# Local attention layers on one core: split norms, another order of the stages, and a narrower last MLP unit

## The chip, the cores and the metric

The kernel runs on one core of one Trainium2 chip. Its time is the device time of one execution in microseconds (us). The core has five engines that run side by side and meet only at semaphores: TensorE (PE, matrix products, with its weight loads as PEld), VectorE (DVE), ScalarE (ACT), GpSimd (POOL) and SyncE (SP, which issues transfers). A change of a few microseconds is small here: the three timed runs lie between 1883.65 and 1890.15 us.

## The reference

Four blocks follow one another on x of shape 16x128x256, each a cross attention and a feed-forward part, added to x with a gate. The change is in the feed-forward part of the second block, which is a small transformer of its own: two layers of local attention. It sees x as 16 sequences of 128 rows, which are one window each, so a row attends to itself and the rows before it in its sequence.

```python
def _layer(x, wqkv, qs, ksc, wo, lg, lb, w1, b1, w2, b2):
    h = shift_token(x)                       # second half of the columns comes from the row before
    q, k, v = jnp.split(h @ wqkv, 3, axis=-1)            # 8 heads of 64
    q = l2norm(q) * qs
    k = l2norm(k) * ksc
    q, k = rotary_xpos(q, k)
    o = local_attention(q, k, v)             # scores, masked softmax, values
    x = x + o @ wo
    h = shift_token(x)
    h = (h - mu) / jnp.sqrt(var + 1e-05) * lg + lb
    a, g = jnp.split(h @ w1 + b1, 2, axis=-1)            # 682 columns each
    x = x + (a * jax.nn.gelu(g, approximate=False)) @ w2 + b2
    return x
```

w1's gate and up columns are cut in units of 128, of which there are six; the last holds the 42 columns that are left (682 = 5 x 128 + 42).

## The kernel before

The whole network is one launch; x stays on the chip as `X`, 128 partitions x 16 blocks x 256 columns, in float32. The local layers are one phase, `local_layers` (line 1203 on), with tiles that carry the prefix L1f. A step is one block of 128 rows in one layer: 16 blocks times two layers are N = 32 steps.

The phase is a software pipeline written by hand. Each engine has a list of pieces with offsets, and `rounds` walks over t and calls each piece for step t + offset, in the order of the list; that order is what the engine executes, and semaphores hold it back where data or buffers are missing. Nothing else decides the order. In round t TensorE runs `queries_keys` of step t (two products of 128x512 into the two banks of psQ), `scores` of t-1 (into psS, a mask product and 8 heads), `turn_weights` of t-2 (transposes the softmax weights pr into psP), `values_in` of t, `values` of t-2 (weights times v, into psS bank 0), `turn_hidden` of t-3, `turn_in` of t+1, `output` of t-2 (into psB), `hidden` of t-3 in three groups j of two units (into psQ again, group j in bank j % 2), `down` of t-3 (psB), `shift`, and `turn` of t (transposes the rotated queries and keys, qr, into psP).

Between these, for step t: ScalarE squares the projections (`squares`, line 1472), VectorE sums the squares by head and clamps them (1580), GpSimd takes the power -0.5 (`roots`, 1287), VectorE multiplies (`norms`, 1597), GpSimd multiplies with the sines (`rotate`), VectorE with the cosines, and adds (`rotated`). ScalarE copies the turned queries and keys (`turned`, to qT and kT), and one step later takes the exponentials (`exps`, two groups of four heads, from maxima that VectorE takes in `tops`); VectorE sums them, GpSimd scales them, TensorE turns them, and ScalarE and VectorE copy one half each (`turned_weights`, pT). ScalarE copies the values' result (`outputs`, oT). For the MLP, ScalarE computes the gelu of a unit's gate (`gates`) and VectorE multiplies with the up part (`products`, into hid).

psQ serves the projections and the hidden units in turn, so the norms of step t must have read it before `hidden` of t-3 writes it:

```python
if j < 2:
    pe.wait_ge(s_qn, min(2 * t + 1 + j, 2 * N))
    after(pe, s_act, U * s.n)
else:
    pe.wait_ge(s_act, U * s.n + 2)
```

and `values` writes the psS bank that the exponentials of the next step read:

```python
pe.wait_ge(s_exp, min(2 * s.n + 3, 2 * N))
```

## Time and profile before

| | |
|---|---|
| Median of 3 runs | 1885.05 us (1883.65 to 1890.15) |
| Profiled execution | 1893.94 us, span 1892.1 us |
| Busy | PE 1654.8 (87%), PEld 1321.2 (70%), DVE 1128.7 (60%), ACT 955.8 (51%), POOL 908.8 (48%) |
| Hidden units' matmuls, L1419 | 1536 instructions, 182.0 us, 275 ns each |
| Query, key products, L1349 | 256, 122.2 us, 622 ns |
| Down projection, L1429 | 384, 94.3 us, 380 ns |
| Roots on GpSimd, L1290 | 32, 93.1 us, 2910 ns |
| Products of the MLP, L1631 | 192, 58.6 us, 346 ns |
| Gelu on ScalarE, L1512 | 192, 60.0 us, 364 ns |

The duration of a matmul is longer than its distance to the next, since matmuls are pipelined: what a group costs TensorE is read from the starts of groups. A matmul instruction on float32 stands twice in the trace for each one in the program. The busy share of an engine is its average over phases of different kinds; the local layers are one of them, and the rows below look at this phase alone.

### The profile page before, as it was taken

The page shows a single profiled execution, that of the slowest core. Times are in us where ns is not written, and L with a number is a line of the kernel's source. Part 1 is how long each engine was busy: PE and PEld are TensorE (multiplying, and loading weights), DVE is VectorE, ACT ScalarE, POOL GpSimd, SP SyncE. Part 2 cuts the span into 40 slices and gives each one's busy share as a digit, 9 for nine tenths or more (in the row PEclk, how much of TensorE's full clock was granted, in tenths as well). Part 3 has the DMA queues.
Part 4 walks back from the last instruction along what each step waited for, and adds up shares of the span by engine and source line. Part 5 has one row for each costly group of instructions (what it writes and reads, how often), then busy time and mean ns, then how long its engine had stood idle before and what let it go on. Part 6 is the DMA issues. An engine that isn't in the chain of part 4 may idle for free. (4 is left out here: it accounts for less than half of the span.)

```text
span 1892.1 us, 37858 instructions
## 1 busy us (share of the span) xinstructions
PE 1654.8 (87%) x11810; PEld 1321.2 (70%) x11841; DVE 1128.7 (60%) x3308; ACT 955.8 (51%) x2743; POOL 908.8 (48%) x1064
## 2 busy tenths in 40 slices
PE   6999369959749999999999999879976999939997
PEld 4777258848626777777777777768855888827775
DVE  4787536628745665666666666458864353327775
ACT  3776235514414655555565555357751355517761
POOL 2366545535445554555455455134755244466620
PEclk9999679979979999999999999989997999969999
DMA  4232355545120000000000000022424244332101
GB/s 153 86 118 90 119 169 171 169 168 182 38 99 1 2 1 1 1 1 1 1 1 1 1 1 1 1 75 86 150 105 174 71 128 129 115 111 98 53 7 45
DMA packets 74546, 138.43 MB, mean 73 GB/s; under 512 B 11568, under 2 KB 56880, under 8 KB 71920
## 3 DMA queue, kind: packets, MB, share of 16 engines
q1 hardware_dynamic: 59472, 95.22, 15.8%
q0 software_dynamic: 13728, 39.60, 6.1%
q8 instruction: 102, 1.67, 0.4%
q10 hardware_dynamic: 1152, 1.18, 0.2%
q14 instruction: 92, 0.75, 0.1%
HBM read 85.14 MB, written 50.82 MB: 72 GB/s over the span
## 5 line engine op out<-in xcount | busy, mean ns | idle before, releaser
L1419 PE MATMUL L1f_psQ<-L1f_xT,arena 128*128 128x128 f32 x1536 | 182.0, 275 | 0.9 <-ACT L1f_xT L1495 0.9
L1419 PEld LDWEIGHTS L1f_psQ<-L1f_xT,arena 128*128 128x128 f32 x1536 | 179.1, 192 | 2.8 <-ACT L1f_xT L1495 1.1
L1290 POOL TENSOR_TENSOR L1f_rn<-L1f_ss,L1f_root_c 128x16 f32<-128x16 f32 x32 | 93.1, 2910 | 176.6 <-DVE L1f_ss L1585 176.6
L1886 POOL DMA_INDIRECT outs_L2f<-L2f_tiles_ys,L2f_tiles_spot x79 | 75.4, 955 | 130.3 <-ACT L2f_tiles_ys L2025 130.3
L1305 POOL TENSOR_TENSOR L1f_rot<-L1f_qn,L1f_sinT 128x512 f32<-128x512 f32 x64 | 111.3, 1760 | 44.9 <-DVE L1f_qn L1602 44.9
L1349 PE MATMUL L1f_psQ<-arena,L1f_hT 128*128 128x512 f32 x256 | 122.2, 622 | 0.6 <-ACT L1f_hT L1502 0.6
L1512 ACT ACTIVATE L1f_sg<-L1f_psQ,vec1f 128x128 f32<-128x128 f32 x192 | 60.0, 364 | 121.3 <-PE L1f_psQ L1419 121.1
L1631 DVE SCALAR_TENSOR_TENSOR L1f_hid<-L1f_psQ,vec1f,L1f_sg 128x128 f32<-128x128 f32 x192 | 58.6, 346 | 84.3 <-ACT L1f_sg L1512 83.0
L1295 POOL TENSOR_TENSOR L1f_pr<-L1f_pr,L1f_rs 128x512 f32<-128x512 f32 x64 | 97.4, 1542 | 22.4 <-DVE L1f_rs L1595 22.4
L1583 DVE TENSOR_REDUCE L1f_ss<-L1f_sq 128x16 f32<-128x1024 f32 x32 | 39.0, 1220 | 114.3 <-ACT L1f_sq L1476 114.3
L1886 POOL DMA_INDIRECT outs_L0f<-L0f_tiles_ys,L0f_tiles_spot x79 | 75.8, 959 | 64.8 <-ACT L0f_tiles_ys L2025 64.3
L1476 ACT ACTIVATE L1f_sq<-L1f_psQ 128x512 f32<-128x512 f32 x64 | 38.2, 597 | 122.4 <-PE L1f_psQ L1349 122.4
L1429 PE MATMUL L1f_psB<-arena,L1f_hid 128*128 128x256 f32 x384 | 94.3, 380 | 1.1 <-DVE L1f_hid L1631 1.1
L714 ACT ACTIVATE L3x_pr<-L3x_psS,L3x_nmx 128x128 f32<-128x128 f32 x256 | 73.6, 432 | 32.8 <-DVE L3x_nmx L838 32.8
L1463 ACT ACTIVATE L1f_pr<-L1f_psS,L1f_mx 128x128 f32<-128x128 f32 x256 | 73.5, 382 | 30.4 <-DVE L1f_mx L1559 30.4
L2095 DVE COPY L2f_tiles_xT<-L2f_tiles_psT 128x256 f32<-128x256 f32 x79 | 33.5, 424 | 92.4 <-PE L2f_tiles_psT L1935 92.4
L1349 PEld LDWEIGHTS L1f_psQ<-arena,L1f_hT 128*128 128x128 f32 x256 | 51.3, 202 | 52.7 <-issue 50.2
L1946 PE MATMUL L0f_tiles_psH<-arena,L0f_tiles_xT 128*128 x316 | 83.8, 388 | 0.2 <-issue 0.2
L1965 PE MATMUL L2f_tiles_psY<-arena,L2f_tiles_aT 128*128 x316 | 81.4, 380 | 1.4 <-ACT L2f_tiles_aT L2019 1.4
L714 ACT ACTIVATE L0x_pr<-L0x_psS,L0x_nmx 128x128 f32<-128x128 f32 x256 | 74.8, 414 | 14.2 <-DVE L0x_nmx L838 14.1
L1946 PE MATMUL L2f_tiles_psH<-arena,L2f_tiles_xT 128*128 x316 | 81.4, 380 | 0.2 <-issue 0.2
L714 ACT ACTIVATE L2x_pr<-L2x_psS,L2x_nmx 128x128 f32<-128x128 f32 x256 | 75.4, 424 | 8.2 <-DVE L2x_nmx L838 8.2
(487 smaller groups left out, 4625.1 us busy)
## 6 DMA issues: line engine op xcount, KB each, us to landing
L0f_tiles_xs<-rows_L0f SPq DMA_DIRECT2D x79, 144.0 KB
L2f_tiles_xs<-rows_L2f SPq DMA_DIRECT2D x79, 144.0 KB
arena<-in_w_L2f SPq DMA_DIRECT2D x8, 1120.0 KB
arena<-in_w_L1f SPq DMA_DIRECT2D x8, 1088.0 KB, 7.4
L1x_got<-outs_L0f SPq DMA_DIRECT2D x16, 512.0 KB, 3.8
L3x_got<-outs_L2f SPq DMA_DIRECT2D x16, 512.0 KB, 3.6
arena<-in_w_L0f SPq DMA_DIRECT2D x8, 768.0 KB, 4.8
rows_L2f<-zero SPq DMA_DIRECT2D x31, 144.0 KB
```

The costliest lines, as they stand in the source:

```text
L714: ins = nc.scalar.activation(pr[:, s.p, g, j * P:(j + 1) * P], psS[:, g, j * P:(j + 1) * P], ACT.Exp, bias=nmx[:, s.p, 4 * g + j:4 * g + j ...
L1290: nc.gpsimd.tensor_tensor(rn[:, s.p], ss[:, s.p], root_c[:, :], ALU.pow).then_inc(s_rn, 1)
L1295: nc.gpsimd.tensor_tensor(a, a, rs[:, s.p, 4 * r:4 * r + 4].unsqueeze(2).broadcast_to([P, 4, P]), ALU.mult).then_inc(s_scaled, 1)
L1305: nc.gpsimd.tensor_tensor(to[:, :, i], of[:, :, o], sin, ALU.mult).then_inc(s_rot, 1)
L1349: mm = nc.tensor.matmul(out, hT[:, s.p, k], part(s, k * 3 * INNER + j * INNER, INNER), start=(k == 0), stop=(k == KC - 1))
L1419: mm = nc.tensor.matmul(out, w, xT[:, k], start=(k == 0), stop=(k == KC - 1), skip_group_check=True)
L1429: mm = nc.tensor.matmul(psB[:, 0:D], hid[:, u], part(s, UNITS_AT + u * UNIT_GLU + 2 * D, D), start=(u == 0), stop=(u == U - 1), skip_group ...
L1463: ins = nc.scalar.activation(pr[:, s.p, r, k * P:(k + 1) * P], psS[:, r, k * P:(k + 1) * P], ACT.Exp, bias=mx[:, s.p, h:h + 1])
L1512: nc.scalar.activation(sg[:, u], psQ[:, j % 2, 2 * i * P:(2 * i + 1) * P], ACT.Gelu, bias=column(s, 2 * KC + u)).then_inc(s_sg, 1)
L1886: nc.gpsimd.indirect_dma_start(r.outs, bass.IndirectOffsetOnAxis(spot[:, t % YR:t % YR + 1], 0), ys[:, t % YR], None).then_inc(r.s_out[t % ...
L1946: mm = nc.tensor.matmul(psH[:, t % 2, 0:W], xT[:, t % 2, k * P:(k + 1) * P], c.arena[:, bass.ds(cols[t] + (first + k * W), W)], start=(k = ...
L1965: mm = nc.tensor.matmul(psY[:, t % 2, 0:D], aT[:, t % 2, i * P:(i + 1) * P], c.arena[:, bass.ds(cols[t] + (first + 2 * W + i * D), D)], st ...
```

## The change

Four things change in the phase, and nothing outside it but the layout of the weights of the last unit.

The norms are taken in two halves: squares, their sums, the clamp, the roots and the multiplication run for the queries (w = 0) and the keys (w = 1) by themselves, with two semaphore counts a step where there was one.

The lists are reordered. TensorE starts a round with turning the weights and the scores, and the query and key projections come third. The lists of ScalarE and VectorE follow.

The result of the values is split: heads 0 to 3 go to psS, heads 4 to 7 to the first 256 columns of psB, and ScalarE copies each as it comes. `values` therefore also waits until VectorE has read the down projection's sum in psB.

The last unit's 42 gate and 42 up columns are packed in one block of 128 columns, gate from column 0 and up from column 64, so one product gives the gate in the partitions 0 to 63 and up in 64 to 127. ScalarE writes the gelu to the upper partitions, VectorE multiplies there, and the down projection reads 64 partitions. That product goes to psQ's bank 1, the other bank than that of unit 4, and has a semaphore count of its own.

```diff
+    LOWER, UPPER = slice(0, P // 2), slice(P // 2, P)
...
+    def unit_bank(u):
+        return 1 if u == U - 1 else u // 2 % 2
+
+    def unit_out(u, m, of=slice(0, P)):
+        at = 2 * (u % 2) * (u < U - 1) + m
+        return psQ[of, unit_bank(u), at * P:(at + 1) * P]
...
-            def roots(s):
-                pool.wait_ge(s_ss, 2 * s.n + 2)
+            def roots(s, w):
+                h = slice(w * LH, (w + 1) * LH)
+                pool.wait_ge(s_ss, 4 * s.n + 2 * w + 2)
                 after(pool, s_qn, 2 * s.n - 2)
-                nc.gpsimd.tensor_tensor(rn[:, s.p], ss[:, s.p], root_c[:, :], ALU.pow).then_inc(s_rn, 1)
+                nc.gpsimd.tensor_tensor(rn[:, s.p, h], ss[:, s.p, h], root_c[:, 0:LH], ALU.pow).then_inc(s_rn, 1)
...
-                after(pe, s_oT, s.n - 1)
+                after(pe, s_oT, 2 * s.n - 2)
...
             def values(s):
                 pe.wait_ge(s_exp, min(2 * s.n + 3, 2 * N))
                 pe.wait_ge(s_vx, s.n + 1)
+                after(pe, s_done, s.n - 1)
                 for k in range(4):
+                    to = psS[:, 0] if k < 2 else psB[:, :]
                     for r in range(2):
                         if k == 0:
                             pe.wait_ge(s_pT1 if r else s_pT0, s.n + 1)
                         h = 2 * k + r
-                        mm = nc.tensor.matmul(psS[64 * r:64 * r + 64, 0, k * P:(k + 1) * P], v[:, s.n % 3, h * LD:(h + 1) * LD],
+                        mm = nc.tensor.matmul(to[64 * r:64 * r + 64, (k % 2) * P:(k % 2 + 1) * P], v[:, s.n % 3, h * LD:(h + 1) * LD],
                                               pT[:, r, k * P:(k + 1) * P], start=True, stop=True, skip_group_check=True)
-                mm.then_inc(s_pv, 1)
+                    if k % 2:
+                        mm.then_inc(s_pv, 1)
...
-                pe.wait_ge(s_oT, s.n + 1)
+                pe.wait_ge(s_oT, 2 * s.n + 2)
...
                 if j < 2:
                     pe.wait_ge(s_qn, min(2 * t + 1 + j, 2 * N))
                     after(pe, s_act, U * s.n)
-                else:
-                    pe.wait_ge(s_act, U * s.n + 2)
                 for i in range(2):
-                    for m in range(2):
-                        out = psQ[:, j % 2, (2 * i + m) * P:(2 * i + m + 1) * P]
+                    if j == 2:
+                        pe.wait_ge(s_act, U * s.n + 2 + 2 * i)
+                    for m in range(1 if 2 * j + i == U - 1 else 2):
+                        out = unit_out(2 * j + i, m)
                         for k in range(KC):
                             w = part(s, UNITS_AT + (2 * j + i) * UNIT_GLU + (m * KC + k) * P, P)
                             mm = nc.tensor.matmul(out, w, xT[:, k], start=(k == 0), stop=(k == KC - 1), skip_group_check=True)
-                mm.then_inc(s_h, 1)
+                    if i == 1 or j == 2:
+                        mm.then_inc(s_h, 1)
...
-                    mm = nc.tensor.matmul(psB[:, 0:D], hid[:, u], part(s, UNITS_AT + u * UNIT_GLU + 2 * D, D),
+                    of = UPPER if u == U - 1 else slice(0, P)
+                    mm = nc.tensor.matmul(psB[:, 0:D], hid[of, u], part(s, UNITS_AT + u * UNIT_GLU + 2 * D, D)[of],
                                           start=(u == 0), stop=(u == U - 1), skip_group_check=True)
...
-            rounds([(queries_keys, 0), (scores, -1), (turn_weights, -2), (values_in, 0), (values, -2), (turn_hidden, -3),
+            rounds([(turn_weights, -2), (scores, -1), (queries_keys, 0), (values_in, 0), (values, -2), (turn_hidden, -3),
...
-            def squares(s):
-                after(act, s_ss, 2 * s.n)
-                for w in range(2):
-                    act.wait_ge(s_qk, 2 * s.n + w + 1)
-                    nc.scalar.activation(sq[:, w], psQ[:, w], ACT.Square).then_inc(s_sq, 1)
+            def squares(s, w):
+                after(act, s_ss, 4 * (s.n - 1) + 2 * w + 2 if s.n else 0)
+                act.wait_ge(s_qk, 2 * s.n + w + 1)
+                nc.scalar.activation(sq[:, w], psQ[:, w], ACT.Square).then_inc(s_sq, 1)
...
             def outputs(s):
-                act.wait_ge(s_pv, s.n + 1)
                 after(act, s_out, s.n)
-                nc.scalar.activation(oT[:, :].rearrange("p k t -> p (k t)"), psS[:, 0], ACT.Copy).then_inc(s_oT, 1)
+                for i, of in enumerate((psS[:, 0], psB[:, :])):
+                    act.wait_ge(s_pv, 2 * s.n + i + 1)
+                    nc.scalar.activation(oT[:, 2 * i:2 * i + 2].rearrange("p k t -> p (k t)"), of[:, 0:2 * P], ACT.Copy).then_inc(s_oT, 1)
...
-                act.wait_ge(s_h, 3 * s.n + j + 1)
                 for i in range(2):
                     u = 2 * j + i
-                    nc.scalar.activation(sg[:, u], psQ[:, j % 2, 2 * i * P:(2 * i + 1) * P], ACT.Gelu,
-                                         bias=column(s, 2 * KC + u)).then_inc(s_sg, 1)
+                    act.wait_ge(s_h, 4 * s.n + j + 1 + i * (j == 2))
+                    to, of = (UPPER, LOWER) if u == U - 1 else (slice(0, P), slice(0, P))
+                    nc.scalar.activation(sg[to, u], unit_out(u, 0, of), ACT.Gelu,
+                                         bias=column(s, 2 * KC + u)[of]).then_inc(s_sg, 1)
...
-            def squares(s):
-                dve.wait_ge(s_sq, 2 * s.n + 2)
-                after(dve, s_rn, s.n - 1)
-                nc.vector.tensor_reduce(ss[:, s.p], sq[:, :].rearrange("p w (h d) -> p (w h) d", d=LD), AXX, ALU.add).then_inc(s_ss, 1)
-                dve.wait_ge(s_ss, 2 * s.n + 1)
-                nc.vector.tensor_scalar(ss[:, s.p], ss[:, s.p], 1e-24, None, ALU.max).then_inc(s_ss, 1)
+            def squares(s, w):
+                h = slice(w * LH, (w + 1) * LH)
+                dve.wait_ge(s_sq, 2 * s.n + w + 1)
+                after(dve, s_rn, 2 * s.n - 2)
+                nc.vector.tensor_reduce(ss[:, s.p, h], sq[:, w].rearrange("p (h d) -> p h d", d=LD), AXX, ALU.add).then_inc(s_ss, 1)
+                dve.wait_ge(s_ss, 4 * s.n + 2 * w + 1)
+                nc.vector.tensor_scalar(ss[:, s.p, h], ss[:, s.p, h], 1e-24, None, ALU.max).then_inc(s_ss, 1)
...
-                dve.wait_ge(s_sg, U * s.n + 2 * j + 2)
                 for i in range(2):
                     u = 2 * j + i
-                    nc.vector.scalar_tensor_tensor(hid[:, u], psQ[:, j % 2, (2 * i + 1) * P:(2 * i + 2) * P], column(s, 2 * KC + U + u),
-                                                   sg[:, u], ALU.add, ALU.mult).then_inc(s_act, 1)
+                    dve.wait_ge(s_sg, U * s.n + (u + 1 if j == 2 else 2 * j + 2))
+                    of, m = (UPPER, 0) if u == U - 1 else (slice(0, P), 1)
+                    nc.vector.scalar_tensor_tensor(hid[of, u], unit_out(u, m, of),
+                                                   column(s, 2 * KC + U + u)[of], sg[of, u], ALU.add, ALU.mult).then_inc(s_act, 1)
...
+def glu_half_unit(gate, up, down):
+
+    n, h = gate.shape[1], P // 2
+    assert n <= h
+    gap = ((0, 0), (0, h - n))
+    both = np.concatenate([np.pad(gate, gap), np.pad(up, gap)], axis=1)
+    return np.concatenate([chunks(both), chunks(np.zeros_like(both)), np.pad(down, ((h, h - n), (0, 0)))], axis=1)
```

The first place is the order on TensorE from one round's projections to its output. Before, the names being psP for turned tiles, psS for scores and values, psA for the value projection, psQ for queries and keys:

```order
L1349 MATMUL L1f_psQ<-arena,L1f_hT 128x512 x4
L1328 MATMUL L1f_psS<-causal,ident 128x512 x2
L1333 MATMUL L1f_psS<-L1f_kT,L1f_qT 128x128 x8
L1344 MATMUL L1f_psP<-consts,L1f_pr 128x128 x8
L1349 MATMUL L1f_psA<-arena,L1f_hT 128x512 x2
L1370 MATMUL L1f_psS<-L1f_pT,L1f_v 64x128 x8
L1391 MATMUL L1f_psA<-consts,L1f_hn 128x128 x2
L1402 MATMUL L1f_psA<-consts,L1f_Y 128x128 x2
L1383 MATMUL L1f_psB<-arena,L1f_oT 128x256 x4
L1419 MATMUL L1f_psQ<-L1f_xT,arena 128x128 x16
```

Now, down to the same hidden groups:

```order
L1353 MATMUL L1f_psP<-consts,L1f_pr 128x128 x8
L1337 MATMUL L1f_psS<-causal,ident 128x512 x2
L1342 MATMUL L1f_psS<-L1f_kT,L1f_qT 128x128 x8
L1358 MATMUL L1f_psQ<-arena,L1f_hT 128x512 x4
L1358 MATMUL L1f_psA<-arena,L1f_hT 128x512 x2
L1381 MATMUL L1f_psS<-L1f_pT,L1f_v 64x128 x4
L1381 MATMUL L1f_psB<-L1f_pT,L1f_v 64x128 x4
L1403 MATMUL L1f_psA<-consts,L1f_hn 128x128 x2
L1414 MATMUL L1f_psA<-consts,L1f_Y 128x128 x2
L1395 MATMUL L1f_psB<-arena,L1f_oT 128x256 x4
L1431 MATMUL L1f_psQ<-L1f_xT,arena 128x128 x16
```

The turned weights and the scores have moved ahead of the four projection matmuls, and the eight products of the values are four into psS and four into psB.

The second place is the end of a round on TensorE: first down products, the shift, the third hidden group, the turn, the rest of down. Before:

```order
L1429 MATMUL L1f_psB<-arena,L1f_hid 128x256 x2
L1438 MATMUL L1f_psA<-L1f_Y,consts 128x128
L1419 MATMUL L1f_psQ<-L1f_xT,arena 128x128 x8
L1447 MATMUL L1f_psP<-consts,L1f_qr 128x128 x8
L1429 MATMUL L1f_psB<-arena,L1f_hid 128x256 x4
L1349 MATMUL L1f_psQ<-arena,L1f_hT 128x512 x4
```

Now:

```order
L1443 MATMUL L1f_psB<-arena,L1f_hid 128x256 x2
L1452 MATMUL L1f_psA<-L1f_Y,consts 128x128
L1431 MATMUL L1f_psQ<-L1f_xT,arena 128x128 x6
L1461 MATMUL L1f_psP<-consts,L1f_qr 128x128 x8
L1443 MATMUL L1f_psB<-arena,L1f_hid 128x256 x4
L1353 MATMUL L1f_psP<-consts,L1f_pr 128x128 x8
```

The third hidden group has six products where it had eight; the rest is as it was.

The third place is ScalarE's start of a round. Before (sq are the squares, pr the exponentials, pT the turned weights, v the values, oT their result):

```order
L1519 ACTIVATE L1f_kT<-L1f_psP 128x512
L1476 ACTIVATE L1f_sq<-L1f_psQ 128x512 x2
L1463 ACT_TABLE_LOAD
L1463 ACTIVATE L1f_pr<-L1f_psS,L1f_mx 128x128 x4
L1470 ACTIVATE L1f_pT<-L1f_psP 128x512
L1486 ACTIVATE L1f_v<-L1f_psA 128x512
L1481 ACTIVATE L1f_oT<-L1f_psS 128x512
L1495 ACTIVATE L1f_xT<-L1f_psA,vec1f 128x128 x2
```

Now:

```order
L1534 ACTIVATE L1f_kT<-L1f_psP 128x512
L1484 ACTIVATE L1f_pT<-L1f_psP 128x512
L1477 ACT_TABLE_LOAD
L1477 ACTIVATE L1f_pr<-L1f_psS,L1f_mx 128x128 x4
L1489 ACTIVATE L1f_sq<-L1f_psQ 128x512
L1477 ACTIVATE L1f_pr<-L1f_psS,L1f_mx 128x128 x4
L1489 ACTIVATE L1f_sq<-L1f_psQ 128x512
L1500 ACTIVATE L1f_v<-L1f_psA 128x512
L1495 ACTIVATE L1f_oT<-L1f_psS 128x256
L1495 ACTIVATE L1f_oT<-L1f_psB 128x256
```

The copy of the turned weights has moved from behind the exponentials to the head of the round, the squares stand one by one around the second group of exponentials, and that group has moved ahead of the values. The table loads are as many as before.

`norms` is split as `squares` is. VectorE's list follows in the same way: both maxima come first, and the sums, the clamp and the norms stand twice, in halves, with the weights' sums between them.

## Rows read from the trace of the kernel before

**Rows 1.** Busy time by stretch, two rounds: stretch, length, engines, clock, DMA.

```profile
607.55:628.30 20.75, 20.37 (x136) 15.67 (x136) 13.07 (x27) 11.75 (x28) 12.63 (x11) 1.00 0.00 1
...
1167.99:1188.54 20.55, 19.95 (x134) 15.27 (x134) 13.62 (x27) 11.82 (x27) 10.83 (x9) 1.00 0.00 1
```

**Rows 2.** Order of time, TensorE, one round: start, length, engine, line, operation.

```profile
898.17 3.60 PE L1349 MATMUL L1f_psQ<-arena,L1f_hT 128*128 128x512 f32 x8
901.82 0.38 PE L1328 MATMUL L1f_psS<-causal,ident 128*128 128x512 bf16 x1
902.13 1.16 PE L1333 MATMUL L1f_psS<-L1f_kT,L1f_qT 64*128 64x128 f32 x16
903.22 1.09 PE L1344 MATMUL L1f_psP<-consts,L1f_pr 128*128 128x128 f32 x8
904.15 1.88 PE L1349 MATMUL L1f_psA<-arena,L1f_hT 128*128 128x512 f32 x4
906.26 1.09 PE L1370 MATMUL L1f_psS<-L1f_pT,L1f_v 128*64 128x128 f32 x16 [0.23 <-ACT L1f_pT L1470]
...
907.57 0.38 PE L1402 MATMUL L1f_psA<-consts,L1f_Y 128*128 128x128 f32 x2
908.05 1.99 PE L1383 MATMUL L1f_psB<-arena,L1f_oT 128*128 128x256 f32 x8
909.88 3.73 PE L1419 MATMUL L1f_psQ<-L1f_xT,arena 128*128 128x128 f32 x32
...
914.53 1.95 PE L1419 MATMUL L1f_psQ<-L1f_xT,arena 128*128 128x128 f32 x16
916.32 1.04 PE L1447 MATMUL L1f_psP<-consts,L1f_qr 128*128 128x128 f32 x8
917.19 1.89 PE L1429 MATMUL L1f_psB<-arena,L1f_hid 128*128 128x256 f32 x8
```

**Rows 3.** Waits from 600 to 1180: total, times, longest.

```profile
PE L1f_psS L1370 <- ACT L1f_pT L1470: 6.6, 28, 0.2
```

**Rows 4.** Order of time, ScalarE and VectorE, the same round.

```profile
900.15 0.60 ACT L1476 ACTIVATE L1f_sq<-L1f_psQ 128x512 f32<-128x512 f32 x1 [2.48 <-PE L1f_psQ L1349]
...
903.77 0.69 DVE L1559 TENSOR_REDUCE L1f_mx<-L1f_psS 128x4 f32<-128x512 f32 x1
...
904.49 1.14 ACT L1463 ACTIVATE L1f_pr<-L1f_psS,L1f_mx 128x128 f32<-128x128 f32 x4 [0.79 <-DVE L1f_mx L1559]
...
905.51 0.61 ACT L1470 ACTIVATE L1f_pT<-L1f_psP 128x512 f32<-128x512 f32 x1
...
907.40 0.60 ACT L1481 ACTIVATE L1f_oT<-L1f_psS 128x512 f32<-128x512 f32 x1 [0.73 <-PE L1f_psS L1370]
...
908.73 0.28 ACT L1501 ACTIVATE L1f_hT<-L1f_psA 128x128 f32<-128x128 f32 x1
```

**Rows 5.** Groups by line and form, GpSimd: count, busy, mean ns, idle before.

```profile
L1290 POOL TENSOR_TENSOR L1f_rn<-L1f_ss,L1f_root_c 128x16 f32<-128x16 f32 x32 | 93.1, 2910 | 176.6 <-DVE L1f_ss L1585 176.6
...
L1313 POOL TENSOR_TENSOR L1f_rf<-L1f_vf,half 128x1 f32<-128x1 f32 x32 | 18.5, 577 | 2.7
...
L1281 POOL TENSOR_TENSOR rstd<-var,half 128x4 f32<-128x4 f32 x4 | 4.1, 1037 | 0.3
```

**Rows 6.** Groups by line and form, VectorE, 600 to 1180.

```profile
L1583 DVE TENSOR_REDUCE L1f_ss<-L1f_sq 128x16 f32<-128x1024 f32 x28 | 34.2, 1220 | 89.1 <-ACT L1f_sq L1476 89.1
```

**Rows 7.** Order of time, GpSimd and VectorE, the same round.

```profile
908.25 3.48 POOL L1305 TENSOR_TENSOR L1f_rot<-L1f_qn,L1f_sinT 128x512 f32<-128x512 f32 x2 [1.40 <-DVE L1f_qn L1602]
...
912.17 3.11 POOL L1295 TENSOR_TENSOR L1f_pr<-L1f_pr,L1f_rs 128x512 f32<-128x512 f32 x2 [0.44 <-DVE L1f_rs L1595]
...
913.17 1.22 DVE L1624 TENSOR_TENSOR L1f_qr<-L1f_cosd,L1f_rot 128x1024 f32<-128x1024 f32 x1
```

**Rows 8.** Order of time, start of the phase.

```profile
548.27 5.14 PE L1349 MATMUL L1f_psQ<-arena,L1f_hT 128*128 128x512 f32 x8
548.51 0.60 ACT L1519 ACTIVATE L1f_kT<-L1f_psP 128x512 f32<-128x512 f32 x1 [0.26 <-PE L1f_psP L1447]
```

More of the change, by code:

```diff
@@ L1313, in hidden_root @@
                 nc.gpsimd.tensor_tensor(rf[:, one], vf[:, one], c.half[:, :], ALU.pow).then_inc(s_rf, 1)
-            rounds([(row_roots, 4), (output_bias, -3), (roots, 0), (rotate, 0), (at(scaled, 0), -1), (at(scaled, 1), -1),
+            rounds([(row_roots, 4), (output_bias, -3), (at(roots, 0), 0), (at(roots, 1), 0), (rotate, 0), (at(scaled, 0), -1), (at(scaled, 1), -1),
                     (hidden_root, -2)])
@@ L1492, in affine @@
                 act.wait_ge(s_T, min(s.n + 5, N))
-                after(act, s_h, 3 * s.n)
+                after(act, s_h, 4 * s.n)
                 for k in range(KC):
@@ L1519, in turned @@
                     nc.scalar.activation(to[:, :].rearrange("p k t -> p (k t)"), psP[:, w], ACT.Copy).then_inc(done, 1)
-            rounds([(squares, 0), (at(exps, 0), -1), (turned_weights, -2), (values_in, 0), (outputs, -2), (affine, -3),
-                    (rows, 1), (at(exps, 1), -1), (gelu_table, -3), (at(gates, 0), -3), (at(gates, 1), -3), (at(gates, 2), -3), (turned, 0)])
+            rounds([(turned_weights, -2), (at(exps, 0), -1), (at(squares, 0), 0), (at(exps, 1), -1), (at(squares, 1), 0), (values_in, 0), (outputs, -2), (affine, -3),
+                    (rows, 1), (gelu_table, -3), (at(gates, 0), -3), (at(gates, 1), -3), (at(gates, 2), -3), (turned, 0)])
         @block.vector
@@ L1563, in turned_weights @@
                 dve.wait_ge(s_pt, 2 * s.n + 2)
-                after(dve, s_pv, s.n)
+                after(dve, s_pv, 2 * s.n)
                 nc.vector.tensor_copy(pT[:, 1], psP[:, 1]).then_inc(s_pT1, 1)
@@ L1595, in sums, with norms @@
                 nc.vector.reciprocal(rs[:, s.p], sm[:, s.p]).then_inc(s_rs, 1)
[L1597 to L1598 removed]
+            def norms(s, w):
                 after(dve, s_rot, 2 * s.n)
                 after(dve, s_cos, s.n)
[L1601 to L1604 removed]
+                dve.wait_ge(s_rn, 2 * s.n + w + 1)
+                nc.vector.tensor_tensor(qn[:, w], psQ[:, w].rearrange("p (h d) -> p h d", h=LH),
+                                        rn[:, s.p, w * LH:(w + 1) * LH].unsqueeze(2).broadcast_to([P, LH, LD]),
+                                        ALU.mult).then_inc(s_qn, 1)
             def output(s):
@@ L1646, in normed @@
                                             ALU.subtract, ALU.mult).then_inc(s_ln, 1)
-            rounds([(row_stats, 4), (results, -4), (squares, 0), (at(tops, 0), -1), (turned_weights, -2), (at(tops, 1), -1),
-                    (norms, 0), (at(weight_sums, 0), -1), (cosines, 0), (output, -2), (at(weight_sums, 1), -1),
-                    (sums, -1), (at(products, 0), -3), (rotated, 0),
+            rounds([(row_stats, 4), (results, -4), (turned_weights, -2), (at(tops, 0), -1), (at(tops, 1), -1), (at(squares, 0), 0),
+                    (at(weight_sums, 0), -1), (at(squares, 1), 0), (at(norms, 0), 0), (at(weight_sums, 1), -1), (sums, -1),
+                    (at(norms, 1), 0), (cosines, 0), (output, -2), (at(products, 0), -3), (rotated, 0),
                     (at(products, 1), -3), (shifted, -2), (at(products, 2), -3), (normed, -2), (rows, 2)])
@@ L2259, in layout @@
             [chunks(f["L1_ffn_wqkv"][n]), chunks(f["L1_ffn_wo"][n])]
-            + [glu_unit(w1[:, HID + a:HID + b], w1[:, a:b], w2[a:b]) for a, b in cuts], axis=1)
+            + [(glu_half_unit if b - a <= P // 2 else glu_unit)(w1[:, HID + a:HID + b], w1[:, a:b], w2[a:b]) for a, b in cuts],
+            axis=1)
+        half = np.zeros(P // 2, np.float32)
+        b_up = np.concatenate([b1[:cuts[-1][0]], half, b1[cuts[-1][0]:HID]])
+        b_up = np.pad(b_up, (0, UNITS1 * P - len(b_up)))
         d[f"col_L1f{n}"] = np.concatenate([columns(f["L1_ffn_ln_g"][n]), columns(f["L1_ffn_ln_b"][n]),
-                                           columns(np.pad(b1[HID:], (0, pad))), columns(np.pad(b1[:HID], (0, pad)))], axis=1)
+                                           columns(np.pad(b1[HID:], (0, pad))), columns(b_up)], axis=1)
         d[f"row_L1f{n}"] = np.concatenate([f["L1_ffn_b2"][n], f["L1_ffn_q_scale"][n], f["L1_ffn_k_scale"][n]])
```

10 lines of the change are left out of this document (2 added, 8 removed).

## The prediction

> **What bounds the kernel now.** The change touches one phase only, the local layers, which fill the span from about 529 to 1230 us. I read it from the outside in. First the busy time by stretch: a round of this phase, one step of each stage on different row blocks, takes 20.75 us, and TensorE is busy in 20.37 us of it at full clock (1.00), while VectorE is busy 13.07, ScalarE 11.75 and GpSimd 12.63 us [rows 1]. Then the order of time on TensorE alone [rows 2]: the starts of its groups add up to the round with hardly a gap, so every matmul taken away shortens the round, and a change on the other engines counts only where TensorE stands before it. Then the waits: the view names one that TensorE still has in every round, 0.23 us before the values' matmuls [rows 3]; a second shows in the starts of rows 2, before the output projection. Last, what the other engines do around these two [rows 4], and how long the operations take that the change splits [rows 5, 6]. Round 4 starts at 607.55 and the last full round ends at 1188.54 [rows 1]: 28 rounds in this steady state.
>
> **The change on TensorE, part by part.**
> (1) The last unit of the MLP has 42 of 128 columns in use. Its gate and up columns now share one block, so that unit needs one product where it had two. A float32 product over two chunks is 4 matmul instructions. The third hidden group has 16 of them, from 914.53 to 916.32, 0.112 us each [rows 2]; 12 remain: -0.45 us. The down projection of that unit reads 64 partitions in place of 128, but as many instructions of as many columns (8 in 1.73 us, 0.215 each), so I give it no gain.
> (2) The wait before the values. The four instructions of the value projection start at 904.15 and take 0.43 each (8 took 3.44, from 898.17 to 901.61), so TensorE could go on at 905.87; it goes on at 906.26 [rows 2], 0.39 later. What it waits for is pT, which ScalarE copies at 905.51, behind the four exponentials of 904.49 [rows 4]. In the new order TensorE turns the weights first, ScalarE copies them first, and scores and query/key products (1.61 + 3.44 us) lie between the turn and the values. That wait goes: -0.39 us.
> (3) The wait before the output projection. The turn of 907.57 has two instructions of 0.11, done at 907.79; the output starts at 908.05, when oT (907.40 to 908.00) is out [rows 2, 4]. With oT in halves, the first is copied while the second half of the products runs. Price of a half: 128x128 takes 0.28 and 128x512 takes 0.60 [rows 4], so some 0.39. The second half starts 1.14 us after the values' start as the whole does now and ends 0.39 later in place of 0.60: -0.2 us, and about 0.05 of the wait stays.
> (4) An added cost. The down projection's last product now has a 64-row form between 128-row ones. The trace has such a change already: the last mask product starts at 901.82 and is over after 0.215, at 902.03, but the 64-row scores start at 902.13, 0.10 later; the way back to 128 rows (903.22) shows no gap [rows 2]. I add 0.10; the ends are 0 and 0.33.
> The Trainium skill ("TensorEngine Tiling (Array Packing)", Key Properties) says that changing the tiling mode drains the engine. A full drain would be what a 256-column product lasts over its spacing, 0.379 less 0.215, so 0.165 us on the way in and as much on the way out. The trace shows 0.10 and nothing; by that rule the sum below would be 6 us smaller, and it is the second case.
> Sum of a round: -0.45 - 0.39 - 0.20 + 0.10 = -0.94 us, 19.81 in place of 20.75.
>
> **Do the other engines keep up with 19.8?** I set the new round at 0 where the weights are turned, with the spacings of rows 2: scores 0.93, queries and keys 2.54, values' projection 5.98, values 7.70, output 9.26, hidden one and two 11.09 (32 instructions of 0.112: 3.57), third hidden 15.74, turn 17.08, rest of down 17.95, end 19.8. Scores are done 1.68 after their start, 2.61. The two maxima take 0.69 each [rows 4], to 3.95. Exponentials one: 3.4 to 4.5. The first square can start 1.98 after its product starts (898.17 to 900.15), at 4.5, the second at 6.2; exponentials two lie between. The reductions of 512 columns take what a maximum takes, 0.69, or half of the 1.22 of now [rows 6], and the clamp is a small one: they land at about 6.1 and 7.65.
> The root of 8 columns is in no row. Roots of 1, 4 and 16 columns take 0.575, 1.04 and 2.91 us [rows 5], a straight line of about 0.42 + 0.155 a column, so 1.65 for 8; the ends are 1.04 and 2.91. With 1.65 the roots are out at 7.9 and 9.5, and the second norm at 10.3. Norms one and two are wanted by hidden one (11.09) and two (12.9): slack 2.5 us and more. Rotation (3.48) runs 10.4 to 13.9 [rows 7]. The sum of 1.22 stands behind the first products and starts now 3.29 after hidden one (913.17 against 909.88), so 14.4 to 15.6, and the turn wants it at 17.08: slack 1.4. The second products are over some 0.7 later, at 16.3; the last unit, alone in the other bank, wants them after its neighbour's 8 instructions, at 16.65: slack 0.35, the tightest place. The weights' scaling (3.11) ends at 17.0 for a turn at 19.8, and kT's copy at about 19.0. The values' first wait, the exponentials one, is over at 4.5 for 7.7. VectorE's busy time grows by two small instructions and stays near 13.5, ScalarE's and GpSimd's below 13: none of them can be the bound by its load, only by its order.
>
> **Start and end of the phase.** In rounds 0 to 3 the chain projection, squares, roots, norms, rotation, turn sets the time, with TensorE idle most of it. The split takes from this chain one half reduction (0.55), one root less a half (2.91 - 1.65 = 1.26) and one norm (0.6): 2.4 us a round. But scores now stand ahead of the projections, and they need kT, which is copied only at 548.51 to 549.11, where the next projection starts at 548.27 [rows 8]: about 0.9 for kT and 1.6 to 2.5 for the scores (the clock is half there) from round 1, and 1 to 2 more for the weights' turn from round 2. That is -2.4, about +0.5, +2 and +2: I count 0, with 3 us either way. In the three rounds after 1188.54 the 0.45 of part 1 comes three times, the wait does not (the exponentials are just as late): -1.3.
>
> **Sum.** 28 x 0.94 = 26.3, plus 1.3, is 27.6, so 28 us off. The profiled execution took 1893.94 us (span 1892.1), 8.9 above the median of 1885.05; the rest of the program is unchanged, and the same 28 us come off both: 1866 for a profile, 1857 for the median.
>
> **Rivals.**
> - Part of it is lost at the 64-row form: 0.33 in place of 0.10 a round, saving 0.71 x 28 + 1.3 = 21: 1864. For it: only one such change could be read, and the new one comes between long products. Against: the gap there is 0.10.
> - The change doesn't do what it says, since the wait moves on: xT is made behind two copies in place of one (slack 0.8 to hidden one), the last unit stands behind the second products (0.35), kT at the new head of the round (0.8). One of them late beyond its slack by half a microsecond or more leaves 0 to 0.45 a round: 1872 to 1885. For it: three slacks under 1 us, each at the end of several estimates. Against: the matmuls that go are gone in any case.
> - Slower: the roots. If 8 columns cost as much as 16 (2.91), both roots end at 12.0, the second norm at 12.7, rotation at 16.2, the sum at 17.5, the second products at 18.2, and the last unit's product waits from 16.65 until then: 1.55 us more than the 0.94 gained, so +0.6 x 28 = +17: 1902. It decides from 2.1 us a root (the slack of 0.35 and the 0.5 by which rotation ends before the sum starts, over two roots), and no gain is left from 2.55. For it: GpSimd's operations have a fixed part that the trace shows only through fits. Against: the 4-column root at 1.04.
> - More than I count: the ramp's chains gain (2.4 us x 4) and the 64-row weights load beside the running product: 1850.
>
> **How the numbers follow.** Forecast 0.68, its own range 1852 to 1863; 64-row form 0.10; moved wait 0.10; slower 0.07; more 0.05. A measurement here tells about 0.3% (5.7 us) from no change. Faster is the first two, the last and half of the moved wait: 0.88; the other half of it, 0.05, is no change; slower 0.07. The range 1849 to 1870 leaves out the slower case and most of the moved wait.
>
> **What would show it.** Right: rounds of about 19.8 us, TensorE busy over 98% of them; 12 instructions in the third hidden group; no idle time before the values; the output's start within 0.1 us of the turn's end; roots of 128x8 at 1.6 to 1.7 us; scores 0.93 us behind the turned weights. Wrong: a wait of TensorE for hid or kT, a root above 2.1 us, a gap over 0.2 us around the last down product, or rounds 1 to 3 longer by more than 2 us each.

## The result and the profile after

The changed kernel takes 1875.40 us (median of 5 runs, 1870.42 to 1876.58) against 1885.05 (5 runs by now, 1883.65 to 1890.15). The ratio of the two is 0.9925, with a 95% interval of 0.9906 to 0.9943: faster by 14 us (11 to 18). The two medians alone lie 9.7 us apart. By the one it is half of the 28 forecast, by the other a third, and both are outside the range of 1849 to 1870. The profiled executions differ by 17.3 us (span 1892.1 and 1874.8), of which 16.0 lie between the first projection of the local layers and the first matmul of the next phase (704.4 and 688.4 us). Outside the phase, where nothing was changed, the profile after is 3.3 us longer ahead of it and 4.6 us shorter behind it. So a difference of a few microseconds in the whole time says little, and the change is read from the phase.

Busy time in a round of the changed kernel, columns as in [rows 1]:

```profile
613.61:633.80 20.19, 20.19 (x134) 15.11 (x133) 13.50 (x28) 12.30 (x29) 13.10 (x11) 1.00 0.00 1
```

A round is 20.19 us in place of 20.75, and TensorE is busy throughout: 20.19 of 20.19. The view of waits names no wait of TensorE between 600 and 1160 us; the 0.23 before the values [rows 3] is gone. So by its records TensorE never stands idle now, and still the round is not the 19.81 of the forecast. The order of time on TensorE says where it is, against [rows 2]:

```profile
896.27 1.09 PE L1353 MATMUL L1f_psP<-consts,L1f_pr 128*128 128x128 f32 x8
897.20 0.59 PE L1337 MATMUL L1f_psS<-causal,ident 128*128 128x512 bf16 x2
897.72 1.16 PE L1342 MATMUL L1f_psS<-L1f_kT,L1f_qT 64*128 64x128 f32 x16
898.81 3.70 PE L1358 MATMUL L1f_psQ<-arena,L1f_hT 128*128 128x512 f32 x8
902.35 1.88 PE L1358 MATMUL L1f_psA<-arena,L1f_hT 128*128 128x512 f32 x4
904.16 0.66 PE L1381 MATMUL L1f_psS<-L1f_pT,L1f_v 128*64 128x128 f32 x8
...
905.19 0.44 PE L1403 MATMUL L1f_psA<-consts,L1f_hn 128*128 128x128 f32 x2
905.46 0.38 PE L1414 MATMUL L1f_psA<-consts,L1f_Y 128*128 128x128 f32 x2
905.74 1.99 PE L1395 MATMUL L1f_psB<-arena,L1f_oT 128*128 128x256 f32 x8
907.57 3.73 PE L1431 MATMUL L1f_psQ<-L1f_xT,arena 128*128 128x128 f32 x32
...
912.23 1.50 PE L1431 MATMUL L1f_psQ<-L1f_xT,arena 128*128 128x128 f32 x12
913.57 1.04 PE L1461 MATMUL L1f_psP<-consts,L1f_qr 128*128 128x128 f32 x8
914.44 2.09 PE L1443 MATMUL L1f_psB<-arena,L1f_hid 128*128 128x256 f32 x8
916.46 1.09 PE L1353 MATMUL L1f_psP<-consts,L1f_pr 128*128 128x128 f32 x8
```

What counts are the distances from one start to the next, in us:

| Stretch | Before | After | Difference |
|---|---|---|---|
| Turned weights | 0.93 | 0.93 | 0 |
| Mask and scores | 1.61 | 1.61 | 0 |
| Queries and keys | 3.44 | 3.54 | +0.10 |
| Values' projection, to the values' start | 2.11 | 1.81 | -0.30 |
| Values | 1.03 | 1.03 | 0 |
| The turns into psA, to the output's start | 0.76 | 0.55 | -0.21 |
| Output, hidden one and two, first down, shift | 6.48 | 6.49 | 0 |
| Third hidden group | 1.79 | 1.34 | -0.45 |
| Turn | 0.87 | 0.87 | 0 |
| Rest of down | 1.73 | 2.02 | +0.29 |
| Sum | 20.75 | 20.19 | -0.56 |

(The sums are of the starts; single entries are rounded.) The rest of down has as many matmuls as before, of as many columns, and takes 0.29 us more. What happens there shows on the weight loads of the same place:

```profile
895.64 0.29 PEld L1443 LDWEIGHTS L1f_psB<-arena,L1f_hid 64*128 64x128 f32 x2 [0.33 <-issue]
896.26 0.86 PEld L1353 LDWEIGHTS L1f_psP<-consts,L1f_pr 128*128 128x128 f32 x8 [0.33 <-issue]
```

The 64-row loads of the last unit come 0.33 us after the end of the load before them, and the next 128-row load comes 0.33 us after the end of those. The profile puts no engine to these gaps, and hid was long done: VectorE's last two products stand at 893.66 to 894.40. A gap alone proves little, since the loads of the 512-column products stand 0.24 apart too. What differs is that both loads here start with their own matmul (895.64 and 896.26, the matmuls at 895.64 and 896.27). In the dense stream elsewhere a load starts while the matmul before its own still runs.

The matmuls of that place one by one, each from a window that holds only it:

```profile
895.33 0.38 PE L1443 MATMUL L1f_psB<-arena,L1f_hid 128*128 128x256 f32 x1
895.64 0.48 PE L1443 MATMUL L1f_psB<-arena,L1f_hid 64*128 64x256 f32 x1
895.96 0.38 PE L1443 MATMUL L1f_psB<-arena,L1f_hid 64*128 64x256 f32 x1
896.27 0.33 PE L1353 MATMUL L1f_psP<-consts,L1f_pr 128*128 128x128 f32 x1
```

Instructions of 256 columns otherwise start 0.215 apart. Here the distances are 0.31, 0.32 and 0.31, and the second of the transposes starts 0.16 behind the first (at 896.43), where the others of its group are 0.11 apart. So each change of form delays two starts: the first instruction of the new form by 0.10, and the second by 0.10 as well, or 0.05 where it is a transpose of 128 columns. That makes 0.29 in the rest of down and 0.05 in the group behind it.

Roots of 8 columns on GpSimd:

```profile
L1299 POOL TENSOR_TENSOR L1f_rn<-L1f_ss,L1f_root_c 128x8 f32<-128x8 f32 x56 | 92.8, 1658 | 178.5 <-DVE L1f_ss L1601 177.4
```

1.66 us each, where 1.65 was read off the line through [rows 5].

The start of the phase went the other way: it became longer. From the first projection to the end of round 3 it takes 81.5 us (532.11 to 613.61) in place of 78.7 (528.81 to 607.55). The end, from the end of round 31 to the next phase, takes 41.6 us in place of 44.6. With 28 rounds of 0.56: +2.8 - 15.7 - 3.0 = -16.0, the whole of the phase's difference.

### The profile page after: what moved, and what is told of

It is laid out like the page before. It is cut to its first block and busy times, and to the rows that moved or that the text cites. A ratio compares the mean times of both kernels' runs of the same rounds, so it can differ in the third digit from the quotient of the medians.

```text
span 1874.8 us, 37913 instructions
## 1 busy us (share of the span) xinstructions
PE 1658.0 (88%) x11713; PEld 1311.1 (70%) x11713; DVE 1144.0 (61%) x3372; ACT 974.5 (52%) x2775; POOL 922.1 (49%) x1096
## 3 DMA queue, kind: packets, MB, share of 16 engines
q8 instruction: 101, 1.65, 0.4%
## 5 line engine op out<-in xcount | busy, mean ns | idle before, releaser
L1299 POOL TENSOR_TENSOR L1f_rn<-L1f_ss,L1f_root_c 128x8 f32<-128x8 f32 x64 | 105.9, 1656 | 213.0 <-DVE L1f_ss L1601 211.8
L1431 PE MATMUL L1f_psQ<-L1f_xT,arena 128*128 128x128 f32 x1408 | 167.7, 275 | 0.9 <-ACT L1f_xT L1509 0.9
L1431 PEld LDWEIGHTS L1f_psQ<-L1f_xT,arena 128*128 128x128 f32 x1408 | 164.8, 192 | 2.8 <-ACT L1f_xT L1509 1.1
L1443 PE MATMUL L1f_psB<-arena,L1f_hid 128*128 128x256 f32 (+1 forms) x384 | 99.7, 388 | 0.0
L1358 PEld LDWEIGHTS L1f_psQ<-arena,L1f_hT 128*128 128x128 f32 x256 | 47.4, 195 | 53.0 <-issue 48.5
L1599 DVE TENSOR_REDUCE L1f_ss<-L1f_sq 128x8 f32<-128x512 f32 x64 | 43.9, 686 | 56.2 <-ACT L1f_sq L1489 56.2
L1443 PEld LDWEIGHTS L1f_psB<-arena,L1f_hid 128*128 128x128 f32 (+1 forms) x384 | 65.2, 190 | 15.6 <-issue 9.6
```

The lines of the kernel that those rows point to most:

```text
L1299: nc.gpsimd.tensor_tensor(rn[:, s.p, h], ss[:, s.p, h], root_c[:, 0:LH], ALU.pow).then_inc(s_rn, 1)
L1358: mm = nc.tensor.matmul(out, hT[:, s.p, k], part(s, k * 3 * INNER + j * INNER, INNER), start=(k == 0), stop=(k == KC - 1))
L1431: mm = nc.tensor.matmul(out, w, xT[:, k], start=(k == 0), stop=(k == KC - 1), skip_group_check=True)
L1443: mm = nc.tensor.matmul(psB[:, 0:D], hid[of, u], part(s, UNITS_AT + u * UNIT_GLU + 2 * D, D)[of], start=(u == 0), stop=(u == U - 1), skip_ ...
```

## The experiments

Two theories stand for the missing 0.38 us a round. A: TensorE loses the early load of its weights each time that it changes between products with 64 and with 128 rows or columns of weights, and the narrow unit's 64-row product adds two such changes. B: that product waits for its own data, the last gelu and product, which cross from one half of the partitions to the other. Eight kernels were run in two groups, each beside the kernel before on its own chip. The kernel before has a median of 1870.78 us in the first group (full rows, the old order with 64 rows, the norms in one piece, the old start) and 1871.95 in the second (the other four). So ratios count and not times across chips, and an expected time that starts from 1875 is some 14 us too high for these chips.

**Full rows.** The last unit's down product reads all 128 partitions; the lower half is zero.

```diff
+            nc.gpsimd.memset(hid[LOWER, U - 1], 0.0).then_inc(s_one, 1)
-                    of = UPPER if u == U - 1 else slice(0, P)
-                    mm = nc.tensor.matmul(psB[:, 0:D], hid[of, u], part(...)[of],
+                    mm = nc.tensor.matmul(psB[:, 0:D], hid[:, u], part(...),
```

(Arguments of `part` left out; the memset has a semaphore count of its own, which the engines wait for at the start.)

> The changed kernel, with the last unit's down product over all 128 partitions (the lower half of hid for that unit is set to zero once), so TensorE never leaves the 128-row form there. Theory A (each change between the 64-row and the 128-row form keeps the next weight load from going ahead): the rest of down is back from 2.02 to 1.73 us and the turn of the weights behind it from 0.93 to 0.87; a round is 20.19 - 0.29 - 0.06 = 19.84 us, 28 rounds give 9.8 us, the time is some 10 to 11 us under the changed kernel's 1875, so 1865. Rival B (the product waits for the last unit's own gelu and product, which come late): the rows in use change nothing, a round stays 20.19 and the time 1875. Rival C (my forecast's price, 0.10 for the form): round 20.09, time 1872.

Measured: 1847.62 us, ratio 0.9875 (0.9860 to 0.9891). TensorE in order of time:

```profile
881.14 1.89 PE L1443 MATMUL L1f_psB<-arena,L1f_hid 128*128 128x256 f32 x8
882.87 1.04 PE L1354 MATMUL L1f_psP<-consts,L1f_pr 128*128 128x128 f32 x8
...
900.12 1.04 PE L1461 MATMUL L1f_psP<-consts,L1f_qr 128*128 128x128 f32 x8
900.99 1.89 PE L1443 MATMUL L1f_psB<-arena,L1f_hid 128*128 128x256 f32 x8
```

The rest of down is 1.73 again (881.14 to 882.87), a round 19.85 (881.14 to 900.99), as theory A said to 0.01. So the 64-row form costs 0.34 us a round in the changed kernel. The phase is 10.2 us shorter than there (678.2 and 688.4), and the two ratios, 0.9875 and 0.9925, lie some 9 us apart, where 10 to 11 were expected. The gelu and product of the last unit are unchanged and cross the partitions as before, so theory B falls.

**The narrow unit in the old order**, with 64 rows and with full rows: the kernel before with only the last unit changed.

> The kernel before with the narrow last unit alone (one product for gate and up, down over 64 rows), old order, norms whole. Theory A: a round is 20.75 - 0.45 + 0.29 = 20.59 us, so 4 to 6 us under the kernel before. Rival C (0.10 for the form): 20.40, 10 us under it. Rival B (a late last unit): near 20.6 too, but with a wait of TensorE on hid in the waits.

Measured, one run: 1869.72 us, where the runs of the kernel before lie between 1868.83 and 1873.14; the 4 to 6 us that were expected did not come. TensorE:

```profile
886.57 1.50 PE L1427 MATMUL L1f_psQ<-L1f_xT,arena 128*128 128x128 f32 x12
887.91 1.04 PE L1457 MATMUL L1f_psP<-consts,L1f_qr 128*128 128x128 f32 x8
888.78 2.09 PE L1439 MATMUL L1f_psB<-arena,L1f_hid 128*128 128x256 f32 x8
890.80 3.70 PE L1357 MATMUL L1f_psQ<-arena,L1f_hT 128*128 128x512 f32 x8
...
894.86 1.16 PE L1341 MATMUL L1f_psS<-L1f_kT,L1f_qT 64*128 64x128 f32 x16
```

Against [rows 2]: third hidden group 1.34 (-0.45), rest of down 2.02 (+0.29), projections with mask, to the scores, 4.06 in place of 3.96 (+0.10). A round is 20.70, so the narrow unit by itself gives 0.05 us of its 0.45 (3.4 us over the phase, 701.0 and 704.4). I had expected 20.59: that the projections behind the 64-row product lose another 0.10 was not in it. A wait of TensorE for hid, the sign of theory B, stands in 2 rounds only, 0.5 us in all.

> The kernel before with the narrow last unit alone, and its down product over all 128 partitions. Theory A (the change of form eats the narrow unit's gain): the 0.45 us come through, a round is 20.30 us where the same with 64 rows had 20.70, so some 13 us under the kernel before, 0.7%. If something else in the narrow unit costs (its gelu across partitions, its own waits), the round stays near 20.7.

Measured: 1857.64 us, ratio 0.9927 (0.9907 to 0.9947). The rounds:

```profile
881.38 1.89 PE L1439 MATMUL L1f_psB<-arena,L1f_hid 128*128 128x256 f32 x8
883.11 3.60 PE L1358 MATMUL L1f_psQ<-arena,L1f_hT 128*128 128x512 f32 x8
...
887.07 1.16 PE L1342 MATMUL L1f_psS<-L1f_kT,L1f_qT 64*128 64x128 f32 x16
```

The rest of down takes 1.73, the projections 3.44, to the scores 3.96; a round is 20.31 (20.33 in the mean of rounds 5 to 31), as expected. The same unit that was worth 0.05 us a round with 64 rows is worth 0.44 with 128, half of them zeros, and 0.7% of the time.

**Two units with 64 rows.** In the changed kernel, unit 2's down product too reads its upper half only. Unlike the last unit, unit 2 has values in its lower half, and this kernel leaves them out of the sum; it serves for the time alone.

```diff
-                    of = UPPER if u == U - 1 else slice(0, P)
+                    of = UPPER if u in (2, U - 1) else slice(0, P)
```

> The changed kernel with a second 64-row product in each down projection: unit 2's too reads only its upper 64 partitions (the lower half of that unit's sum is left out). As many matmuls of as many columns. Theory A: one more stretch in the 64-row form costs what the first does, 0.3 us before a 128-row weight load of a like group, so a round is 20.19 + 0.29 = 20.48 us, and the rest of down takes 2.31. Rival (the 0.29 belongs to the end of the round, or to the last unit's data): 20.19.

Measured: a round of 20.58, 0.39 more than the changed kernel, where 0.29 were expected; the one timed run took 1875.49 us, beside 1871.95 for the kernel before.

```profile
890.42 1.04 PE L1461 MATMUL L1f_psP<-consts,L1f_qr 128*128 128x128 f32 x8
891.39 2.38 PE L1443 MATMUL L1f_psB<-arena,L1f_hid 64*128 64x256 f32 x8
893.71 1.09 PE L1353 MATMUL L1f_psP<-consts,L1f_pr 128*128 128x128 f32 x8
```

The rest of down is 2.32, as expected, and the turn ahead of it 0.97 in place of 0.87. Read one by one, unit 2's product delays four starts by 0.10 each: its own two (891.39, which lengthens the turn, and 891.71) and the first two of the 128-row form behind it (892.02 and 892.34). I expected 0.29 since I had counted the rest of down alone; the fourth delay falls in the group behind, where it is 0.05 to 0.06 on the last unit's transposes and 0.10 on unit 3's products. So the cost comes again with a second product in another place, and the 0.29 belongs neither to the end of the round nor to the last unit's data. Two 64-row products side by side were not tried: no run separates the number of changes from the number of 64-row products. Both products also read the upper half, so nothing here tells whether a lower half would cost the same.

**Norms in one piece.** The changed kernel with sums, roots and norms whole, behind the second square.

```diff
-            rounds([..., (at(roots, 0), 0), (at(roots, 1), 0), (rotate, 0), ...
+            rounds([..., (roots, 0), (rotate, 0), ...
-  (at(weight_sums, 0), -1), (at(squares, 1), 0), (at(norms, 0), 0), (at(weight_sums, 1), -1), (sums, -1), (at(norms, 1), 0),
+  (at(weight_sums, 0), -1), (squares, 0), (at(weight_sums, 1), -1), (sums, -1), (norms, 0),
```

> The changed kernel with sums, roots and norms in one piece again, behind the second square. If the split is what keeps the norms off TensorE's path in the new order: the norms end 0.8 us after the first hidden group wants its bank, a round is 20.19 + 0.85 = 21.0 us and the time about 1895 to 1900, over the kernel before. Rival (there is slack enough, the split pays only at the start): round 20.19, 5 to 7 us more in rounds 0 to 3.

Measured, one run: 1931.06 us, 60 over the kernel before; a round is 22.42, where 21.0 was expected. VectorE, then TensorE:

```profile
895.30 1.29 DVE L1616 TENSOR_TENSOR L1f_qn<-L1f_psQ,L1f_rn 128x512 f32<-128x512 f32 x2 [2.20 <-POOL L1f_rn L1298]
...
900.24 2.05 DVE L1638 TENSOR_TENSOR L1f_qr<-L1f_cosd,L1f_rot 128x1024 f32<-128x1024 f32 x1 [0.69 <-POOL L1f_rot L1313]
```

```profile
893.35 1.99 PE L1394 MATMUL L1f_psB<-arena,L1f_oT 128*128 128x256 f32 x8
896.10 3.81 PE L1430 MATMUL L1f_psQ<-L1f_xT,arena 128*128 128x128 f32 x32 [0.75 <-issue]
...
900.83 1.06 PE L1430 MATMUL L1f_psQ<-L1f_xT,arena 128*128 128x128 f32 x8
902.86 0.71 PE L1430 MATMUL L1f_psQ<-L1f_xT,arena 128*128 128x128 f32 x4 [0.97 <-DVE L1f_hid L1646]
```

The norms end at 896.59, and the hidden groups start at 896.10, after the first of the two, in place of some 895.2: 0.9 lost. (The profile writes "issue" at this wait; that it is for the norms is read from the program and from the times.) The sum for the turned queries and keys then waits for rotation, the second products stand behind it on VectorE, and the last unit waits another 1.15 for them (901.71 to 902.86). I expected the first wait (0.85) and not the second. The split of the norms, which takes no work from TensorE, is what carries the new order: without it the rest of the change is 1.67 us a round slower than the kernel before.

**Values in one bank.** The kernel with full rows, with the values' result in one bank and its copy whole.

> The kernel with full rows, with the values' result in one bank and one copy again. If halving the copy is what took 0.20 us from the wait before the output projection: a round is 19.85 + 0.20 = 20.05 us, with the output's start 0.48 after the turn's in place of 0.28. Rival (the copy is early anyway, since ScalarE has less to do there in the new order): 19.85.

Measured, one run: 1851.13 us, a round of 20.06, 0.21 more than with full rows and as expected. TensorE and ScalarE:

```profile
891.24 0.38 PE L1412 MATMUL L1f_psA<-consts,L1f_Y 128*128 128x128 f32 x2
891.73 1.99 PE L1393 MATMUL L1f_psB<-arena,L1f_oT 128*128 128x256 f32 x8
```

```profile
890.04 0.60 ACT L1496 ACTIVATE L1f_v<-L1f_psA 128x512 f32<-128x512 f32 x1 [1.06 <-PE L1f_psA L1359]
891.08 0.60 ACT L1491 ACTIVATE L1f_oT<-L1f_psS 128x512 f32<-128x512 f32 x1 [0.44 <-PE L1f_psS L1380]
```

The output starts 0.49 after the turn again, at the end of one copy of 0.60. The halves are worth 0.21 us a round.

**The old order in rounds 0 to 3.** Full rows, and for t < 4 the lists of the kernel before on TensorE, ScalarE and VectorE, with the norms split.

```diff
-                for fn, off in pieces:
+                for fn, off in (first if first and t < 4 else pieces):
```

> As the kernel with full rows, and in rounds 0 to 3 the pieces of TensorE, ScalarE and VectorE stand in the order of the kernel before (the norms stay split). The changed kernel needs 81.5 us from the first projection to the end of round 3, the one before 78.7. Theory S (the scores and the turned weights ahead of the projections lengthen the start): 81.5 falls to 71 to 76, below the one before, since the split norms take 2.4 us out of each chain; the time is 5 to 9 us under the kernel with full rows. Rival T (the start is longer by chance of the clock, which is half there): no change beyond 1 us.

Measured: 1834.62 us, ratio 0.9816 (0.9802 to 0.9829). In the changed kernel the first rounds go like this on TensorE:

```profile
547.44 1.97 PE L1461 MATMUL L1f_psP<-consts,L1f_qr 128*128 128x128 f32 x8 [5.98 <-DVE L1f_qr L1639]
550.18 1.01 PE L1337 MATMUL L1f_psS<-causal,ident 128*128 128x512 bf16 x2 [0.78 <-ACT L1f_kT L1534]
551.12 2.08 PE L1342 MATMUL L1f_psS<-L1f_kT,L1f_qT 64*128 64x128 f32 x16
553.13 4.47 PE L1358 MATMUL L1f_psQ<-arena,L1f_hT 128*128 128x512 f32 x8
```

Between the turn and the projections stand a wait of 0.78 for kT and 2.95 us of mask and scores, which take 1.61 in the steady rounds. TensorE has been idle for 6 us before, and the granted clock of these 2.95 us is 0.50, the lower of its two levels of 1.2 and 2.4 GHz, where the steady rounds have 1.00:

```profile
550.18:553.13 2.95, 2.95 (x18) 1.90 (x18) 0.00 (x0) 0.00 (x0) 0.00 (x0) 0.50 0.00 0
```

With the old start, in order of time:

```profile
534.97 1.97 PE L1461 MATMUL L1f_psP<-consts,L1f_qr 128*128 128x128 f32 x8 [5.98 <-DVE L1f_qr L1644]
536.73 4.57 PE L1359 MATMUL L1f_psQ<-arena,L1f_hT 128*128 128x512 f32 x8
541.35 0.38 PE L1338 MATMUL L1f_psS<-causal,ident 128*128 128x512 bf16 x1
```

The projections follow the turn at once. It is they that now run in part at the lower clock (0.79 on average from 536.73 to 541.35), and the scores behind them have 1.00. To the end of round 3 it takes 71.2 us (519.79 to 591.02) in place of the changed kernel's 81.5, and 7.5 less than the kernel before: the split norms shorten the chain there, as forecast, and the new order had cost all of that and 2.8 more. Theory S holds, and rival T, which allowed no more than 1 us, falls.

The time fell by more than the start explains: 13.0 us by the medians of the two kernels with full rows, 11 by their ratios, where 5 to 9 were expected. The profiles show 8.5 us in the phase (678.2 and 669.7); the rest lies outside it, where the two kernels are the same, and is not explained.

**Scores ahead of the turned weights**, on top of that.

> The kernel with full rows and the old start, with the scores ahead of the turned weights, so that the group behind the 64-row scores is the transposes (which take 0.93 there and 0.87 elsewhere) and not the projections (3.54 there and 3.44 elsewhere). Theory A: 0.10 - 0.06 = 0.04 us a round, 19.81, 1 us in all, which the time can't tell but the rounds can. Rival (exponentials and squares come too late, since ScalarE's first copy now stands behind them): a round over 20 us with a wait for hid or pT.

Measured: 1835.19 us, ratio 0.9810 (0.9792 to 0.9828), so the same as the last; the round is 19.80 where it was 19.85, and 19.81 was expected. No wait of TensorE appears. TensorE:

```profile
889.37 1.09 PE L1354 MATMUL L1f_psP<-consts,L1f_pr 128*128 128x128 f32 x8
890.30 3.60 PE L1359 MATMUL L1f_psQ<-arena,L1f_hT 128*128 128x512 f32 x8
893.73 1.88 PE L1359 MATMUL L1f_psA<-arena,L1f_hT 128*128 128x512 f32 x4
```

The projections are back at 3.43, and the turned weights, now behind the scores, take 0.93 where they took 0.87. So a group of transposes behind the scores is 0.06 longer, and a group of 512-column products there 0.10.

The last two kernels take 1.8% to 1.9% off the kernel before, where the change took 0.75%; their phase is 34.7 and 38.0 us shorter than before, against 16.0.

## Why the prediction was wrong

**Step 4, the price of the 64-row form, failed.** The prediction put it at 0.10 us a round, and the runs show 0.34: with full rows the round falls from 20.19 to 19.85. It took the 0.10 from the one change of form that it read, into the scores [rows 2], where it saw only the first late start, and it read the way out as free. One by one, the second score also starts late there (902.34 behind 902.13, 0.21, where the later pairs are 0.11 apart). On the way out the first of the turned weights stands 0.21 behind the last pair of scores (903.01 and 903.22), and the second 0.17 behind the first. "The way back to 128 rows shows no gap" was the mistake: a late start does not show as idle time, since a matmul's record is longer than its distance to the next; it is the distance that grows, and the turned weights' 0.93 against the turn's 0.87 for the same number of transposes was there to be read.

The Trainium skill ("TensorEngine Tiling (Array Packing)", Key Properties) says that a change of mode drains the engine. The page gives no duration; the prediction's estimate of a drain in and out from its own rows was 0.33, and the trace agrees in sum, with 0.34, though not in the parts, 0.20 in and 0.15 out for 0.165 each. I had that case with a chance of 0.10, and it would have given 21 us, still more than was measured, so it was not the whole of the miss.

**Step 2 was half right.** The wait for pT went entirely, but the stretch fell by 0.30 and not by 0.39. The values start 0.52 behind the last instruction of their projection (903.64 to 904.16), where those are 0.43 apart, and their load starts with them (904.16). That looks like another such change, into 64 columns, which the wait had covered; no run takes it away, so this 0.09 is read by likeness and not shown by an experiment. The new order has a price that no step had: behind the scores the projections lose 0.10, where the turned weights lost 0.06 before, 0.04 net. The three make the missing 0.24 + 0.09 + 0.04, which is 0.38 but for rounding, 10.6 us in 28 rounds.

**Steps 1 and 3 held**: -0.45 and -0.21. So did the other engines: no wait of TensorE is left, the roots take 1.66, and the price of a 128x256 copy was 0.38. The slower rival needs roots above 2.1 us; they were not, so it did not come. The kernel with whole norms shows that norms which come late do make TensorE wait, which is the way by which that rival would have cost.

**The start**, counted as 0 with 3 us either way, is +2.8, within its bounds. Its terms were -2.4, +0.5, +2 and +2 for rounds 0 to 3, which make 2.1 and not 0. From turn to turn the traces have -2.4, +1.3, +3.6 and 0, and 0.3 behind the last turn for the 64-row form. **The end** gave 3.0 in place of 1.3. By the starts of the two traces, a gap of 0.53 ahead of the last two down products went in each of the three last rounds, since the last group's units are now released one by one; with the form's own cost the rest of down is 0.34 shorter there (2.36 and 2.02), 1.0 in all. The halved copies give 0.2 twice; the last 0.3 was not traced. In all: 10.6 + 2.8 - 1.7 = 11.7 us, the difference between the 27.6 forecast and the 16.0 of the phase. The step from these 16.0 to the 14 of the ratio is within its interval; the 9.7 of the medians is not, and stays unexplained.

## What to carry to other kernels

On a TensorE without idle time, count the changes between products of different row or column extent as work: a product that uses half the rows saved nothing by it here, and its pair of changes in a dense stream cost as much as three float32 instructions of 128 columns (0.34 us against 0.112 each); padding the rows with zeros cost no time in the rounds. Read the cost of a group from the distance to the next start, and compare like groups behind different neighbours. An order that is better in the steady state can be worse for filling the pipeline: give the first rounds a list of their own.
